# Turning the quantised activations with VectorE and a trip through DRAM instead of TensorE, beside causal attention

## What is computed

```python
x = L0_attn_x
xn = _layernorm(x, axis=-1)
x = x + attention(xn, Wqkv, Wout, bout) + gated(xn, w_gate, w_up, w_down)
# attention: 16 heads of 16 channels, causal, softmax over up to 2048 keys
# gated, with fp4_linear(a, w) = fp4(a) @ fp4(w).T :
gate = fp4_linear(x, w_gate)          # 256 -> 704
y = fp4_linear(x, w_up)               # 256 -> 704
h = silu(gate) * y
return fp4_linear(h, w_down)          # 704 -> 256
# fp4: blocks of 16 along the last dimension, scale = max|.| / 6,
# values rounded to 0, 0.5, 1, 1.5, 2, 3, 4, 6 times the scale
```

## Time and profile before

| | |
|---|---|
| median of three runs | 2762.43 us (2761.91 to 2763.21) |
| the profiled execution | 2762.52 us, span of its records 2760.8 us |
| granted TensorE clock, mean | 0.978 |
| busy share of the span: PE, ACT, DVE, POOL | 93%, 74%, 70%, 26% |
| one batch of the main phase | 440 us, four of them from 998 us on |

### The profile page before, as it was taken

How to read it: one execution, slowest core, us unless ns; L and a number is a source line. 1 busy time by engine, 2 the same in 40 slices (tenths; PEclk the granted TensorE clock), 3 DMA queues, 4 the chain that set the end, 5 groups by cost and what they waited for, 6 DMA issues and landing times.

```text
span 2760.8 us, 58289 instructions
## 1 busy us (share of the span) xinstructions
PE 2562.2 (93%) x18228; PEld 1304.5 (47%) x18228; DVE 1934.7 (70%) x5533; ACT 2038.4 (74%) x3502; POOL 722.6 (26%) x550
## 2 busy tenths in 40 slices
PE   2995999999999859999999999999999999999999
PEld 1883444444444424444454444444444445444455
DVE  7995999999999935655645656655656654566555
ACT  1554999999999847777758777775777775777775
POOL 3563334433333221122111112111121111212111
PEclk7997999999999979999999999999999999999999
DMA  2785555555445342202222112123022031220200
GB/s 70 238 272 123 75 75 75 76 72 71 71 70 72 45 84 38 51 19 39 47 78 48 32 31 46 29 58 80 22 42 43 21 76 50 40 47 23 41 24 32
DMA packets 118622, 175.70 MB, mean 64 GB/s; under 512 B 25648, under 2 KB 95024, under 8 KB 117808
## 3 DMA queue, kind: packets, MB, share of 16 engines
q1 hardware_dynamic: 97392, 147.33, 28.6%
q10 hardware_dynamic: 16576, 15.73, 2.1%
q0 software_dynamic: 4352, 8.92, 1.3%
HBM read 129.37 MB, written 42.53 MB: 62 GB/s over the span
## 4 chain that ended last, share of the span: by engine, by line
PE 54%; ACT 4%; issue 4%; SPq 1%; DMA 1%; DVE 0%; ACTq 0%; POOL 0%; DVEq 0%; POOLq 0%
PE O L923 17%; PE S L907 15%; PE F L943 10%; PE F L983 5%; ACT probs L1052 4%; PE F L973 2%; PE S L994 2%; PE S L910 2%; SPq L528 1%; PE F L936 1%; DMA y<-in_L_attn_x_dram 1%; DMA q_st<-s_shift 0%; DVE o_turned L1258 0%; ACTq L1047 0%; ACT xt_hi L1077 0%
## 5 line engine op out<-in xcount | busy, mean ns | idle before, releaser
L1052 ACT ACTIVATE probs<-S 128x1024 f32<-128x1024 f32 (+3 forms) x1280 | 1074.5, 897 | 227.6 <-PE S L910 84.1
L907 PE MATMUL S<-q_st,k_st 128*128 128x512 bf16 (+3 forms) x2560 | 648.8, 351 | 75.0 <-DMA q_st<-s_shift 38.4
L730 ACT ACTIVATE m_excess<-m_DIFF 128x512 f32<-128x512 f32 (+7 forms) x1536 | 647.1, 472 | 88.3 <-PE m_DIFF L690 42.3
L748 DVE CUSTOM_DVE_ANT_0 m_excess<-m_S,m_excess 128x512 f32<-128x512 f32 (+7 forms) x1536 | 700.7, 530 | 11.7 <-PE m_S L690 9.2
L923 PE MATMUL O<-probs,v_sb 128*32 128x512 f32 (+3 forms) x5120 | 603.6, 543 | 2.2 <-POOL v_sb L1129 2.2
L688 PE MATMUL m_S<-m_k,m_q 128*128 128x512 bf16 (+7 forms) x1536 | 483.1, 325 | 26.7 <-DVE m_row_max L748 17.3
L688 PE MATMUL m_DIFF<-m_k,m_q_diff 128*128 128x512 bf16 (+7 forms) x1536 | 478.0, 319 | 29.5 <-DMA m_q_diff<-s_q 29.2
L907 PEld LDWEIGHTS S<-q_st,k_st 128*128 128x128 bf16 x2560 | 213.7, 98 | 418.2 <-ACT probs L1052 235.1
L632 POOL TENSOR_TENSOR m_q_diff<-m_zero,m_q 48x4096 bf16<-48x4096 bf16 x32 | 224.4, 7011 | 429.0 <-DMA m_q<-s_q 418.3
L688 PEld LDWEIGHTS m_S<-m_k,m_q 128*128 128x128 bf16 x1536 | 148.3, 97 | 275.8 <-DVE m_row_max L748 194.9
L1246 DVE TENSOR_TENSOR ht_lo<-F,ht_hi 128x512 fp32r<-128x512 f32 (+1 forms) x128 | 71.0, 557 | 232.5 <-ACT ht_hi L1067 232.5
(11 more groups left out here) (163 smaller groups left out, 4189.8 us busy)
## 6 DMA issues: line engine op xcount, KB each, us to landing
k_st<-s_k SPq DMA_DIRECT2D x96, 256.0 KB, 8.6
q_st<-s_q SPq DMA_DIRECT2D x384, 64.0 KB
s_q<-a_part SPq DMA_DIRECT2D x48, 256.0 KB, 3.0
s_k<-a_part SPq DMA_DIRECT2D x48, 256.0 KB, 2.2
m_q<-s_q SPq DMA_DIRECT2D x96, 128.0 KB, 3.8
m_k<-s_k SPq DMA_DIRECT2D x96, 128.0 KB, 6.7
m_q_diff<-s_q SPq DMA_DIRECT2D x96, 128.0 KB, 8.1
m_k<-s_k SPq DMA_DIRECT2D x96, 124.0 KB, 5.2
```

Of the source, the lines that this page charges most:

```text
L730: act.activation(excess[u % MAX_EXCESS][:, 0:keys // 2], DIFF[u % MAX_BUFS][:, 0:keys // 2], ACT.Relu) \
L748: dve.tensor_tensor_reduce(larger, S[u % MAX_BUFS][:, 0:keys // 2], larger, 1.0, -3e38, ALU.add, ALU.max, column).then_inc(reduced[u % MAX ...
L907: ins = pe.matmul(S[half][:, s % 2, 0:st.width], k_st[p][:, s, st.j * P:(st.j + 1) * P], q_st[st.c % 2][:, s, st.skip:QC], start=True, sto ...
L1052: act.activation(probs[half][st.n % 2][:, :, 0:st.width], S[half][:, :, 0:st.width], ACT.Exp, scale=SCALE).then_inc(exped[half], 1)
```

## The change

The transposes leave PE. DVE turns the quantised tile in 32 x 32 blocks in SBUF (`x_turn` at k = 6 for tile n+1, `h_turn` at k = 4 for tile n-1). SP then stores it to a scratch tensor in DRAM, waits for that store, and loads it back with four DMAs, one for each group of 32 partitions, so that every block lands where the full transpose has it. Both sides of such a piece are 32 values of 4 bytes, 128 bytes: 1024 pieces for x and 3072 for h. ACT copies the high part from SBUF, of x where PE's transpose stood (k = 0), of h in one piece of 768 columns at k = 8. POOL subtracts for the low parts, which DVE did. The down product moves from k = 0 to k = 1 and its addition on DVE to k = 2.

SP's list changes with it. It starts the queries of the next chunk at the first step of the present one, and the trips of h and x stand in the same list at k = 4 and k = 6. The keys and queries of the next batch are loaded ahead of the last h, the values behind it. POOL places the values of a batch behind the first x's quantisation. `FLUSH_DOWN` becomes 12.

```diff
+def unflip(eng, dst, dram, tiles, sem):
+    blocks = dram.rearrange("(a r) (m g s) -> g r m a s", r=SLOT, s=SLOT, g=P // SLOT)
+    for g in range(P // SLOT):
+        rows = dst[g * SLOT:(g + 1) * SLOT, :].rearrange("r (m a s) -> r m a s", m=tiles, s=SLOT)
+        eng.dma_start(rows, blocks[g]).then_inc(sem, 16)
...
+            def turn_h(b, n):
+                sp.wait_ge(q_zeroed, 2)
+                sp.wait_ge(h_flipped, b * tiles + n + 1 + PRIMED)
+                sp.dma_start(dram["h_flip"], h_flip[:, :]).then_inc(h_flip_st, 16)
+                sp.wait_ge(q_zeroed, 2)
+                sp.wait_ge(h_flip_st, b * (16 * tiles) + 16 * (n + 1) + PRIMED)
+                unflip(sp, ht, dram["h_flip"], ITILES, ht_ld)
...
+            def batch(b, more):
+                turn_x(b, 0)
+                for st in steps:
+                    n, k = divmod(st.n, per_tile)
+                    if st.first and st.chunk + 1 < chunks:
+                        load_chunk(b, st.chunk + 1)
+                    if k == 4 and n >= 1:
+                        turn_h(b, n - 1)
+                    elif k == 6 and n + 1 < tiles:
+                        turn_x(b, n + 1)
+                if more:
+                    load_chunk(b + 1, 0)
+                turn_h(b, tiles - 1)
+                if more:
+                    load_batch(b + 1)
...
-                    if k == 0 and n >= 2:
+                    if k == 1 and n >= 2:
                         down(b, n - 2)
-                    if op == "turn":
-                        x_turn(b, n)
-                    elif op == "gate":
+                    if op == "gate":
...
-                    elif k in (8, 9) and n >= 1:
-                        h_turn(b, n - 1, k - 8)
...
+            def h_high(b, n):
+                act.wait_ge(ht_ld, b * (16 * UNFLIP_DMAS * tiles) + 16 * UNFLIP_DMAS * (n + 1) + PRIMED)
+                act.wait_ge(down_ps, b * tiles + n + PRIMED)
+                act.activation(ht_hi[:, :], ht[:, :], ACT.Copy).then_inc(ht_hi_done, 1)
...
+                def h_turn(n):
+                    dve.wait_ge(h_ready, b * tiles + n + 1 + PRIMED)
+                    dve.wait_ge(ht_lo_done, b * tiles + n + PRIMED)
+                    dve.transpose(h_flip[:, :], h_fp4[:, :]).then_inc(h_flipped, 1)
...
-FLUSH_TURN, FLUSH_DOWN = 2, 6
+FLUSH_TURN, FLUSH_DOWN = 2, 12
```

More of the change, by code:

```diff
@@ new lines, in load_chunk @@
+            def load_chunk(b, chunk):
+                hg, c = divmod(chunk, NQC)
+                if c == 0:
+                    load_stack(sp, k_st[hg % 2][:, :, :], dram["k"], K_STACK, hg * HG, HG, bass.ds(b * T, T), group_ld[hg % 2])
+                q = q_st[c % 2]
+                tokens = bass.ds(b * T + c * QC, QC)
+                sp.wait_ge(q_zeroed, 2)
+                sp.wait_ge(o_free[c % 2], b * (chunks // 2) + chunk // 2 + PRIMED)
+                load_stack(sp, q[:, :, :], dram["q"], Q_STACK, hg * HG, HG, tokens, q_ld[c % 2])
+                sp.dma_start(q[STACK:QK_ROWS, :, :],
+                             dram["shift"][:, bass.ds(b * H + hg * HG, HG), c * QC:(c + 1) * QC]) \
+                    .then_inc(q_ld[c % 2], 16)
@@ new lines, in load_batch @@
+            def load_batch(b):
+                sp.wait_ge(q_zeroed, 2)
+                sp.wait_ge(x_rs, b * tiles + PRIMED)
+                sp.dma_start(norm[:, :, :], dram["norm"][:, bass.ds(b * tiles, tiles), :]).then_inc(norm_ld, 16)
+                sp.wait_ge(q_zeroed, 2)
+                sp.wait_ge(y_head_st, b * 16 + PRIMED)
+                for n in range(HEAD_TILES):
+                    sp.dma_start(y[:, n, :], x_rows[bass.ds(b * T + n * P, P), :]).then_inc(y_ld[n % 2], 16)
+                sp.wait_ge(q_zeroed, 2)
+                sp.wait_ge(v_ready, b * NHG + PRIMED)
+                sp.dma_start(v_in[:, :, :], dram["v"][:, bass.ds(b * NKB, NKB), :]).then_inc(v_ld, 16)
@@ L898, in _ @@
+            load_chunk(0, 0)
+            load_batch(0)
+            with sp.Fori(0, B - 1) as b:
+                batch(b, True)
+            batch(B - 1, False)
         @block.tensor
@@ L925, in values @@
                 ins.then_inc(pv_done, 1)
-            def x_turn(b, n):
-                pe.wait_ge(x_ready, b * tiles + n + 1 + PRIMED)
-                if n == 0:
-                    pe.wait_ge(y_final, b * tiles + PRIMED)
-                else:
-                    pe.wait_ge(gate_free, b * 2 * tiles + 2 * n + PRIMED)
-                if n >= 2:
-                    pe.wait_ge(ht_lo_done, b * 2 * tiles + 2 * (n - 1) - 1 + PRIMED)
-                for kk in range(KD):
-                    ins = pe.transpose(F[0][:, kk * P:(kk + 1) * P], x_fp4[:, kk * P:(kk + 1) * P], ident[:, :])
-                ins.then_inc(xt_ps, 1)
             def gated_product(f, name, ch, done):
@@ L1025, in _ @@
                 for m in range(tiles):
-                    if m == FLUSH_TURN:
-                        for part in range(2):
-                            h_turn(b, tiles - 1, part, flush=True)
-                    elif m == FLUSH_DOWN:
+                    if m == FLUSH_DOWN:
                         down(b, tiles - 1)
@@ L1074, in _ @@
                     exps(b, st, 1)
-                    if op == "turn":
-                        act.wait_ge(xt_ps, b * tiles + n + 1 + PRIMED)
-                        act.activation(xt_hi[:, :], F[0][:, 0:KD * P], ACT.Copy).then_inc(xt_hi_done, 1)
+                    if op == "high":
+                        x_high(b, n)
                     elif op == "gate":
                         gate_parts(b, n, ch)
-                    elif k in (8, 9) and n >= 1:
-                        h_high(b, n - 1, k - 8)
+                    if k == 8 and n >= 1:
+                        h_high(b, n - 1)
                     if k == 9 and n + HEAD_TILES < tiles:
@@ L1085, in _ @@
                         load_tile(b, n + HEAD_TILES)
-                for part in range(2):
-                    h_high(b, tiles - 1, part)
+                h_high(b, tiles - 1)
                 for first, last in STORES:
@@ L1167, in _ @@
                 h_rescale(b, tiles - 1)
+                h_low(b, tiles - 1)
         @block.vector
@@ L1310, in _ @@
                 for m in range(tiles):
-                    if m == FLUSH_TURN + 1:
-                        for part in range(2):
-                            h_low(tiles - 1, part)
+                    if m == FLUSH_TURN:
+                        h_turn(tiles - 1)
                     elif m == FLUSH_DOWN + 1:
```

149 lines of the change are left out of this document (67 added, 82 removed).

## The result

The changed kernel takes 2917.07 us (median of four runs, 2913.23 to 2922.35) where the kernel before takes 2762.82. The ratio is 1.056, with a 95% interval of 1.054 to 1.058: slower by 154 us, where 62 were forecast. The profiled execution took 2915.67 us, its span 2913.9.

What follows compares the result with a forecast made beforehand. ACT was taken to set the pace in plain steps, PE's list or both in turn where gated-layer parts are added. 2762.5 - 46 + 78 + 13 + 17 = 2824.5 us, said as 2825, 2.2% slower; range 2747 to 2905.

Steps and rivals of the forecast that it cites:

- parts 1 and 2: Steps 8 and 9 gain 0.5 us a tile, steps 0 and 1 0.27 us: 46 us for 60 tiles.
- The low part on POOL: POOL's subtraction for h takes up to 2.2 us from step 8, wanted some 4 us later; costed at nothing.
- A wait of ACT of any length is passed on in full: Main phase: two score buffers couple PE and ACT, so every ACT wait counts whole; no separate size.
- behind such a trip x's own is just in time: After a late trip of h, x's trip still arrives in time since ACT is later too; no cost given.
- part 3: Step 8: queries ahead of h's trip in SP's list make 28 trips 2.8 us late: 78 us, bounds 48 to 157.
- part 4: Tile 0's later gated product makes x's trip for tile 1 3.3 us late, 4 times: 13 us.
- part 5: Batch ends and starts: 4.6 us for each of three starts, 2 for the first, 1 for the last end: 17 us.
- A: Rival: h's trip is in time behind the queries too; 2747 us, 0.6% faster; chance 0.10.
- B: Rival: PE's transposes cost more, ACT's waits of 107 us at x and 53 at h return; 2692 us; chance 0.05.
- C: Rival: small pieces cost twice, h's trip 9.4 us, 28 trips late by 5.5 and 32 by 1.4; 2955 us; chance 0.15.
- D: Rival: gain and loss cancel within 0.2%, some 5 us, with trips late by 0.5 us; chance 0.05.

Runs made afterwards that it cites:

- no_trip: Changed kernel without the stores to DRAM and loads back; ACT and POOL read DVE's blocks in SBUF, so the output is not the right one: 2747.76 us.
- straight: Changed kernel with each trip's four loads as whole rows instead of 128 B pieces, so the output is not the right one: 2875.86 us.
- spread: Changed kernel with queries behind x's trip, edits at batch edges, next batch's values, keys, queries behind x's trips of tiles 11, 13, 14, last h turned earlier: 2782.97 us.

## Why the prediction was wrong in size

**The gain (parts 1 and 2): -46 forecast.** "Together they are 5.13 us against 3.92 for two plain steps" took every part of the difference as on the path. Steps 8 and 9 did shrink by 0.55 to 1.34 us in no_trip, 0.84 in the mean and more than the forecast's 0.5, but steps 0 and 1, forecast to lose 0.27, grew by 0.15 to 0.66 with x's transposes gone and by 0.64 in most tiles with them kept. So only 0.26 to 0.76 us a tile is left in most tiles: 36 us of 46 for tiles 1 to 15, by no_trip. This error is 10 us; that the second copy and the wait behind it lay beside PE's list of step 0 is my reading of it. The low part on POOL, costed at nothing, was right in the steps: 1.81 us in the groups above, wanted later.

**"A wait of ACT of any length is passed on in full."** This sentence failed: behind a late trip more is lost than the wait. Against no_trip, steps 9, 0 and 1 behind the late trips lose 33 us in the main phase, most of the last line of the ledger. Two causes offer themselves, x's trip, which comes late behind h's, and PE's clock. These windows of after lie at the start of tiles 3, 5, 7 and 9 of the second batch, each behind a late trip; the clock is the column behind POOL.

```profile
1565.00:1573.00 8.00, 6.38 (x42) 3.09 (x44) 2.05 (x5) 6.31 (x8) 6.29 (x6) 1.00 0.18 36
1620.00:1628.00 8.00, 6.64 (x63) 4.27 (x65) 4.09 (x9) 4.85 (x10) 5.20 (x5) 1.00 0.16 36
1674.00:1682.00 8.00, 7.01 (x25) 1.30 (x26) 2.18 (x5) 6.03 (x8) 6.11 (x6) 0.57 0.17 36
1731.00:1739.00 8.00, 6.79 (x51) 4.15 (x53) 3.34 (x6) 4.08 (x8) 5.14 (x5) 0.79 0.17 35
```

The three steps lose 0.0 us in tiles 3 and 5, 2.4 in tile 7 and 1.3 in tile 9, while ACT's wait for `xt` is 0, 0.8, 0 and 0.6 us. All 24 places divide so: 5 with the clock at its upper level lose nothing (0.04 us at most), though ACT waits for `xt` for up to 0.95 us in them; 11 with 3 to 4 us at the lower level lose 1.1 to 1.6 us; 8 with some 7 us at it lose 2.1 to 2.5. In straight, where ACT never waits for `xt` by more than 0.25 us behind a late trip, 13 of the 24 places have the lower level and lose 1.1 to 2.4 us, and the other 11 nothing. So it is the clock: in tile 7 four matmuls of the scores are listed at 1.95 us, and at 1.04 where the clock is back. PE was without work for 2.2 to 3.8 us in all 24, and in 19 of them the lower level followed; what decides it, no run tells. The sentence "behind such a trip x's own is just in time" was off by up to 1 us, and that cost nothing. The forecast has no term for the clock.

**The queue of SP (part 3): right.** ACT waits at step 8, in every tile that I named but tile 14, whose chunk is the last and loads no queries: 24 and not 28. Each makes step 8 longer by 2.9 us than before, and by 3.1 than in no_trip, forecast 2.8. The trip took 7.7 us against 6.7: the store and its waits take 2.9 and not 2.5, the loads land in 2.8 and not 2.4 us and the four issues are 0.7 us apart and not 0.6; the seven issues ahead take 3.3 us, forecast 3.4. The trip's extra 1.0 us is partly made up by luck: SP begins with the queries 7.8 us before ACT is ready, where I had 7.35.

**Tile 0 (part 4): right.** 3.3 us forecast, 3.1 to 3.8 measured at step 0 of tile 1.

**Ends and starts (part 5): 17 forecast, 61 measured,** the step that failed worst. I priced the trips there with the landing times of a quiet stretch. The store of the last h took 3.9 to 5.4 us and not 2.3 in three batches, behind the next batch's keys, which my list of SP's order contained and my sum didn't. That price stood in the trace of the kernel before: 15.2 us for 128 KB behind bulk loads, as shown above, and up to 15.7 in the earlier trace rows. Then the down product waits for POOL's low part (PE 26.9 us, above; 6.5 in no_trip). At the start, the queries of chunk 1 stand behind x's trip, and PE waits for them; in ACT's timeline of after, tile 0 of the third batch:

```profile
1972.12 1.94 ACT L1072 ACTIVATE probs<-S 128x1024 f32<-128x1024 f32 x2 [3.42 <-PE S L961]
```

PE waits so for 2.8 to 3.9 us in each batch, 14.3 in all. That edit I hadn't costed at all: "it starts the queries of the next chunk at the first step of the present one" stands in the change, and chunk 0 has only four steps. And 21 of the 61 us stay in no_trip: there PE waits for the placed values (9.6 us in four places), which I had, and for POOL's low part; the rest of the 21 I didn't trace.

**The rivals.** A (trips in time) is out: from the first of the seven issues, 1719.54, to the landing, 1730.5, it is 11 us, and A needed 7.3 from about there. Its counter-argument "no store or load in this trace lands in less than 2.1 us" was not quite so, loads of y land in 1.9 at best; nothing hangs on it. B is out: no_trip itself has 2748. C is out: the loads land in 2.8 us, 24 trips wait and not 60, and the pieces cost 41 us by straight, where C had 130. D is out with A. The Trainium skill ("DMA: Bandwidth & Descriptors", "Rules for kernel authors") speaks against turning by a plain DMA with a rearranged access pattern. This case agrees that it costs, though less than the order does: whole rows instead of its small pieces save 41 us of the 154, and spread, which keeps the pieces and changes the order, saves 134.

## What to carry to other kernels

A transfer put into a loop has two prices: its own time, and its place behind all bytes already queued by any engine. If it comes late there is a third, the clock of a PE that had to wait. Read the landing time of a small DMA near a bulk load, not its median, and tie bulk loads by a wait to the event that they must follow: a place in an engine's list isn't a time. And a gain in one step can be given back in the next, so it is read over the whole tile.

## What I had not expected of the hardware

- A DMA of 128 KB, issued on ACT's queue 4 us behind 1.5 MB on SP's, landed after 12.5 us instead of 2.1. A store of 384 KB took, instead of 2.3 us, 5.0 with 1.9 MB of keys and queries issued 8 to 15 us ahead of it, 7.5 with as much 2 to 11 us ahead, and 10.3 with 3.9 MB of keys, queries and values 8 to 14 us ahead.
- Four loads of 768 pieces of 128 B, issued some 0.7 us apart, each landed in 2.8 us; whole rows in 2.1. Small pieces were no disaster at this size.
- After 2.2 to 3.8 us without work PE's granted clock was at its lower level of 1.2 GHz for 3 to 7 us in 19 of 24 places and stayed at 2.4 in five. Where it fell, a wait of 3 us cost 1.1 to 2.5 us more than its length; where it didn't, nothing.
- A copy of 128x768 by ACT from SBUF takes 844 ns, and the two copies from PSUM made 990.
- PE time added to this loop cost 85% of itself, and the same time removed, along with other moves, brought half.
